# Four stages of a gated stack reordered: spline normalisation on VectorE, table rows by halves, and first similarities and one-hots taken earlier

## The chip, the cores and the metric

The kernel runs on one core of a Trainium2 chip. The metric is device time in microseconds (us), from the start of the launch to its end. Engines are named as the profile names them: PE (TensorE), PEld (its weight loads), DVE (VectorE), ACT (ScalarE), POOL (GpSimd) and SP (SyncE, which issues most transfers).

## What is computed

A stack of four layers, each with a mixer and a feed-forward block, on x of 8 x 256 x 512 floats. Every block adds tanh(gate) times its result of the layer-normalised x. The change touches the feed-forward of layer 1 (a spline layer), the mixer of layer 3 (a decaying state) and the feed-forward of layer 3 (retrieval by product keys):

```python
# _L1_ffn_ref, N = 2048 tokens, 64 tiles of 8 columns, 8 clusters
input_sigs = jnp.sign(xf)
cluster_scores = input_sigs @ cluster_sigs.T
tile_scores = input_sigs @ tile_sigs.T
tile_idx = jnp.argmax(jnp.where(in_cluster, tile_scores, -jnp.inf), axis=-1)
...
b = spline_bases[tile_idx[:, None], j, gi]
s = spline_slopes[tile_idx[:, None], j, gi]
delta = (b + s * x_local) * output_scale[tile_idx][:, None]
out = jnp.zeros_like(xf).at[jnp.arange(N)[:, None], tok_dims].set(delta)
...
# _L3_xattn_ref, after the scan
y = Z + summary
return (y - mu) / jnp.sqrt(var + LN_EPS) * gamma + beta
...
# _L3_ffn_ref
q = (x @ Wq).reshape(b, t, H, 2, DK)
sim1 = jnp.einsum('bthd,hkd->bthk', q1, keys[:, :, 0, :])
sim2 = jnp.einsum('bthd,hkd->bthk', q2, keys[:, :, 1, :])
s1, i1 = jax.lax.top_k(sim1, K)
...
w_down = e_down[final_indices]
w_up = e_up[final_indices]
hidden = jax.nn.silu(jnp.einsum('btd,bthkd->bthk', x, w_down)) * jax.nn.relu(final_scores)
out = jnp.einsum('bthk,bthkd->btd', hidden, w_up)
```

## The kernel before

The whole of x stays in SBUF as X, 16 tiles of 128 tokens by 512 columns. The kernel is a row of stages, each a function with its own buffers. At the end of a stage all engines meet, so that what is late on any of them delays all. `stats` carries the mean and the squared deviations of each row of X into the next stage. Stages, semaphores and the order on each engine are written out by hand; the order in the code is the order in the queue. `wait_ge(here(i, h))` in a loop means that turn i of buffer h has been filled, `before(i, h)` that its last use is over.

**Spline stage** (`spline_phase`, names with L1f, 596.8 to 718.2 us of the profile). DVE makes the row scale `r2` and shift `nm`. ACT normalises each tile into XN (L1583), four tiles ahead and then one between two sign operations (L1589). PE turns XN in chunks of four 128x128 transposes (L1514), ACT takes the sign of a turned chunk, and PE scores four tiles at a time against the tiles' signatures (L1522, 16 matmuls of 64 columns). DVE makes the one-hot OH of the chosen tile, eight tiles of X at a time (L1663 to L1671), and picks the eight chosen columns of each row, XS. PE turns the one-hots (L1540), ACT copies them to OHT (L1613), PE multiplies them with a table to fetch each token's row (L1546), and ACT copies the row to LUT (L1617); the two PSUM buffers of each are used in turn. PE does all 16 one-hots first, then all 16 rows. DVE's chain from L1683 on waits for the last row and has a long tail. At the end (the put loop) POOL spreads the result of a tile over 512 columns (L1502), DVE adds it to X (L1739) and makes the tile's statistics with bn_stats (L1743). ACT meanwhile is nearly idle.

**Decay stage** (`decay_phase`, L3x, 913 to 960 us). Each tile gets its layer norm, times gamma, plus beta. DVE makes z (L2051) and adds it to X with the row sum as a by-product; POOL has added beta to X before. ACT turns the row sum into the mean (L2004, a 128x2 copy) and then squares the deviations (L2010). PE is idle but for eight matmuls at the start.

**Route stage** (`route_phase`, L3r, 960 to 1098.8 us). DVE makes the row scale and shift of all 16 tiles with ACT's root between. Tiles go in eight pairs: ACT normalises two tiles (L2181), PE turns them, makes queries with Wq (L2155 and on) and similarities with the keys (L2167), ACT copies each result back, DVE takes the best eight of each of 8 rows of similarities (L2234) and goes on to the indices (`choose`). `mask` (L2219) and `keep_keys` (L2225), with POOL's `rank` and products between (L2135, L2139), belong to the pair before. At the end DVE makes the indices, weights `wts`, the statistics `stat`, and transposes FW, PH and PK.

**Retrieve stage** (`retrieve_phase`, L3f, 1099 to 1758 us). DVE splits the weights and x into high and low halves (`up_low` L2602, `down_low` L2598, `split_x` L2594), makes `xs` (L2659), and then one-hots of the chosen indices, 44 times (`one_hots`: one 128x512 compare, L2572, and four 128x128 ones, L2576). PE sums their products (L2419), and then come the hidden layer and the output in a long run of matmuls.

## Time and profile before

| | |
|---|---|
| median of 3 runs | 1764.09 us (1761.99 to 1770.47) |
| the profiled execution's own time | 1760.03 us |
| its span in the trace | 1758.3 us |
| mean granted TensorE clock, as a share of full speed | 0.892 |
| PE busy | 1363.1 us (78%) |
| DVE busy | 1424.3 us (81%) |
| ACT busy | 936.0 us (53%) |
| POOL busy | 545.6 us (31%) |

The busy times are averages over stages with different limits. The stages which the change touches take 121, 47, 139 and 659 us. The page's chain that ended last puts 24% of the span on PE and 6% on DVE, nearly all of it in the retrieve stage, and says nothing of the stages ahead; the rows of the timeline do. A row of the timeline joins instructions of one kind that follow each other on one engine: its duration runs from the first's start to the last's end.

### The profile page before, as it was taken

How to read it: one execution, taken by the hardware profiler on the slowest of the kernel's cores; microseconds unless marked ns; L12 is line 12 of the kernel's file. 1: busy time of each engine (PE TensorE's matmuls, PEld its weight loads, DVE VectorE, ACT ScalarE, POOL GpSimd, SP SyncE). 2: the span in 40 equal slices, each digit the busy share in tenths (PEclk: the TensorE clock that was granted, in tenths of full speed). 3: DMA queues.
4: the chain of work that ended last, by engine and by line, in shares of the span. 5: the costliest groups of instructions: out<-in, count | busy, mean ns of one | idle time of the engine just before them, and what ended most of it. 6: DMA issues, size and time to landing. Idle time of an engine off the chain costs nothing. (4 is left out here: it accounts for less than half of the span.)

```text
span 1758.3 us, 23962 instructions
## 1 busy us (share of the span) xinstructions
PE 1363.1 (78%) x6614; PEld 1011.7 (58%) x6614; DVE 1424.3 (81%) x3156; ACT 936.0 (53%) x1936; POOL 545.6 (31%) x569
## 2 busy tenths in 40 slices
PE   4889358886999667266771992489999899998888
PEld 2444224444788443254620882368888788876776
DVE  5999769985887468799488799888999889878785
ACT  3477646652333362466425441358888788733443
POOL 0000014442110022200013122214777577766541
PEclk8899779998999757688885996799999999999999
DMA  6230020000000210355200100416889799887974
GB/s 213 90 123 13 0 78 1 0 0 1 1 1 1 86 61 1 93 194 179 68 1 0 48 25 1 125 49 208 248 245 251 210 263 256 251 235 234 261 231 157
DMA packets 92286, 197.93 MB, mean 113 GB/s; under 512 B 16040, under 2 KB 25384, under 8 KB 91312
## 3 DMA queue, kind: packets, MB, share of 16 engines
q0 software_dynamic: 27120, 91.25, 18.9%
q1 hardware_dynamic: 65088, 105.82, 18.3%
q14 instruction: 51, 0.42, 0.1%
q8 instruction: 27, 0.44, 0.1%
HBM read 181.30 MB, written 15.73 MB: 112 GB/s over the span
## 5 line engine op out<-in xcount | busy, mean ns | idle before, releaser
L2379 POOL DMA_INDIRECT L3f_gd<-rows,idx x160 | 188.4, 1178 | 202.2 <-DVE L3f_gd L2608 177.0
L2379 POOL DMA_INDIRECT L3f_gu<-in_L_ffn_e_up,idx x160 | 168.4, 1052 | 71.2 <-issue 47.2
L2447 PE MATMUL L3f_o_ps<-L3f_euh,L3f_ath 128*128 128x512 f32 x352 | 146.4, 416 | 22.4 <-DVE L3f_atl L2589 19.5
L2435 PE MATMUL L3f_h_ps<-L3f_xh,L3f_edh 128*128 128x512 f32 (+1 forms) x384 | 144.0, 375 | 6.7 <-DVE L3f_xl L2594 6.7
L2419 PE MATMUL L3f_g_ps<-L3f_oh 128*128 128x128 f32 x704 | 97.0, 282 | 61.5 <-DVE L3f_oh L2576 61.5
L2435 PE MATMUL L3f_h_ps<-L3f_xh,L3f_edl 128*128 128x512 f32 (+1 forms) x384 | 144.0, 375 | 0.0
L2435 PE MATMUL L3f_h_ps<-L3f_xl,L3f_edh 128*128 128x512 f32 (+1 forms) x384 | 143.9, 375 | 0.0
L1030 POOL TENSOR_TENSOR wgu<-L0f_hid,magic 128x1408 bf16<-128x1408 f32 x16 | 45.2, 2825 | 315.2 <-DVE L0f_hid L1101 315.2
L2447 PE MATMUL L3f_o_ps<-L3f_eul,L3f_ath 128*128 128x512 f32 x352 | 138.9, 395 | 0.0
L2447 PE MATMUL L3f_o_ps<-L3f_euh,L3f_atl 128*128 128x512 f32 x352 | 138.9, 395 | 0.0
L2419 PEld LDWEIGHTS L3f_g_ps<-L3f_oh 128*128 128x128 f32 x704 | 90.9, 194 | 72.0 <-issue 67.4
L2622 DVE SCALAR_TENSOR_TENSOR X<-L3f_gu,L3f_coef,X 128x512 f32<-128x512 f32 x160 | 119.4, 747 | 0.7
L2491 ACT ACTIVATE L3f_at<-L3f_h_ps 128x512 f32<-128x512 f32 (+1 forms) x96 | 53.8, 560 | 116.3 <-PE L3f_h_ps L2435 77.7
L2585 DVE TENSOR_TENSOR L3f_at<-L3f_at,L3f_G 128x512 f32<-128x512 f32 (+1 forms) x96 | 62.1, 647 | 63.7 <-ACT L3f_at L2491 52.4
L2608 DVE SCALAR_TENSOR_TENSOR L3f_gd<-L3f_gd,L3f_xs 128x512 f32<-128x512 f32 x160 | 109.4, 685 | 0.0
L2447 PEld LDWEIGHTS L3f_o_ps<-L3f_euh,L3f_ath 128*128 128x128 f32 x352 | 66.8, 190 | 47.6 <-issue 36.8
L2512 ACT ACTIVATE L3f_oh<-L3f_oh,first,L3f_minus 128x128 f32<-128x128 f32 x216 | 89.2, 484 | 1.8
L2435 PEld LDWEIGHTS L3f_h_ps<-L3f_xh,L3f_edh 128*128 128x128 f32 x384 | 73.2, 191 | 18.4 <-DVE L3f_xl L2594 7.7
L2496 ACT ACTIVATE L3f_ath<-L3f_at 128x512 fp32r<-128x512 f32 (+1 forms) x96 | 57.3, 597 | 47.8 <-DVE L3f_at L2585 28.8
L2602 DVE TENSOR_TENSOR L3f_eul<-L3f_eu,L3f_euh 128x512 fp32r<-128x512 f32 x96 | 66.2, 690 | 18.5 <-ACT L3f_euh L2486 14.7
L2435 PEld LDWEIGHTS L3f_h_ps<-L3f_xl,L3f_edh 128*128 128x128 f32 x384 | 72.9, 190 | 10.8
L331 PE MATMUL L0x_vp_ps<-L0x_W,L0x_V 128*128 128x512 f32 x128 | 63.5, 643 | 20.0 <-ACT L0x_sv L491 20.0
(555 smaller groups left out, 3729.3 us busy)
## 6 DMA issues: line engine op xcount, KB each, us to landing
L3f_eu<-in_L_ffn_e_up SPq DMA_DIRECT2D x96, 256.0 KB
L3f_ed<-in_L_ffn_e_down SPq DMA_DIRECT2D x96, 256.0 KB
L2x_ed<-in_L_ffn_e_down SPq DMA_DIRECT2D x32, 256.0 KB, 3.3
rows<-L2x_eo SPq DMA_DIRECT2D x32, 256.0 KB, 2.4
wgu<-in_L_ffn_w_gate_upT SPq DMA_DIRECT2D x4, 1408.0 KB, 7.5
X<-in_x SPq DMA_DIRECT2D x4, 1024.0 KB, 10.2
L0x_V<-in_ctxT SPq DMA_DIRECT2D x8, 512.0 KB, 3.9
L1f_C<-in_ctx SPq DMA_DIRECT2D x2, 2048.0 KB, 12.9
```

Of the source, the lines that this page charges most:

```text
L331: last = pe.matmul(vp_ps[:, :], lhsT=V[b % 3][:, c, j * P:(j + 1) * P], rhs=W[:, c, D:2 * D], start=(c == 0), stop=(c == DC - 1))
L2379: pool.indirect_dma_start(buf[j % ND][:, :], None, table, bass.IndirectOffsetOnAxis(ap=idx[:, j:j + 1], axis=0)).then_inc(sem[j % ND], 16)
L2419: last = pe.matmul(g_ps[h][:, g, :], lhsT=oh2[h][:, g, :], rhs=oh1[h][:, g, :], start=True, stop=True)
L2435: last = pe.matmul(h_ps[h][:, 0:cols], lhsT=w[h][:, c, :], rhs=x[:, c, 0:cols], start=(c == 0 and m == 0), stop=(c == DC - 1 and m == 2))
L2447: last = pe.matmul(o_ps[a][:, :], lhsT=w[h][:, a * P:(a + 1) * P], rhs=x[h][:, :], start=False, stop=False)
L2491: act.activation(at[h][:, 0:cols], h_ps[h][:, 0:cols], ACT.Silu).then_inc(sl_ready, 1)
L2496: act.activation(ath[h][:, 0:cols], at[h][:, 0:cols], ACT.Copy).then_inc(ath_ready, 1)
L2512: last = act.activation(oh1[h][:, g, :], oh1[h][:, g, :], ACT.Relu, scale=minus[:, n * GR + g:n * GR + g + 1], bias=first[:, 1, n * GR + g ...
L2585: dve.tensor_tensor(ah, ah, Ge, ALU.mult).then_inc(at_ready, 1)
L2602: dve.tensor_tensor(eul[h][:, :], eu[h][:, :], euh[h][:, :].bitcast(F32), ALU.subtract).then_inc(eul_ready, 1)
L2608: dve.scalar_tensor_tensor(gd[j % ND][:, :], gd[j % ND][:, :], 1.0, xs[:, j // S, :], ALU.mult, ALU.mult, accum_out=hid[:, j:j + 1]).then_ ...
L2622: dve.scalar_tensor_tensor(X[:, TG + j // S, :], gu[j % ND][:, :], coef[:, j:j + 1], X[:, TG + j // S, :], ALU.mult, ALU.add).then_inc(add ...
```

## The change

Four stages are edited.

In the spline stage, normalising moves from ACT to DVE (a tensor_scalar), eight tiles straight after `nm` and eight after `sigs`. PE turns the first eight one-hots, fetches their rows, and then does the same with the second eight; the second row buffer is now `s_ps`, and ACT's copies follow the same order. In the put loop DVE's addition also gives the row sum; for 15 of the 16 tiles ACT makes the mean of it and squares the deviations, in place of bn_stats; the copy of `mean` stands at tile 8 of that loop.

```diff
-    l_ps = [t[:, :, :].rearrange("p t a -> p (t a)")[:, 0:TW] for t in ts_ps]
+    l_ps = [ts_ps[0][:, :, :].rearrange("p t a -> p (t a)")[:, 0:TW], s_ps[:, 0:TW]]
...
-            i, h = t // 2, t % 2
-            if t % 8 == 0:
-                pe.wait_ge(oh_made, 1 + t // 8)
-            pe.wait_ge(oht_ready, before(i, h))
-            pe.transpose(oh_ps[h], OH[:, t, :], ident[:, :]).then_inc(oh_turned, 1)
         pe.wait_ge(tab_in, 80)
-        for t in range(NT):
-            i, h = t // 2, t % 2
-            pe.wait_ge(oht_ready, here(i, h))
-            pe.wait_ge(lut_ready, before(i, h))
-            pe.matmul(l_ps[h], lhsT=OHT[:, t, :], rhs=TAB[:, :], start=True, stop=True).then_inc(l_ready, 1)
+        for k in range(2):
+            pe.wait_ge(oh_made, 1 + k)
+            for t in range(8 * k, 8 * k + 8):
+                i, h = t // 2, t % 2
+                pe.wait_ge(oht_ready, before(i, h))
+                pe.transpose(oh_ps[h], OH[:, t, :], ident[:, :]).then_inc(oh_turned, 1)
+            for t in range(8 * k, 8 * k + 8):
+                i, h = t // 2, t % 2
+                pe.wait_ge(oht_ready, here(i, h))
+                pe.wait_ge(lut_ready, before(i, h))
+                pe.matmul(l_ps[h], lhsT=OHT[:, t, :], rhs=TAB[:, :], start=True, stop=True).then_inc(l_ready, 1)
         pe.wait_ge(mm_made, 1)
         for k in range(2):
...
-        def normalise(t):
-            act.activation(XN[:, t, :], X[:, t, :], ACT.Identity, scale=r2[:, t:t + 1], bias=nm[:, t:t + 1]).then_inc(xn_ready, 1)
...
             for c in range(DC):
                 signs(g, c)
-                if g + 1 < NT // TG4:
-                    normalise(TG4 * (g + 1) + c)
...
+        for k in range(2):
+            with act.Fori(NP // 2 * k, NP // 2 * (k + 1)) as i:
+                for h in range(2):
+                    act.wait_ge(oh_turned, here(i, h))
+                    act.activation(OHT[:, 2 * i + h, :], oh_ps[h], ACT.Copy).then_inc(oht_ready, 1)
+            with act.Fori(NP // 2 * k, NP // 2 * (k + 1)) as i:
+                for h in range(2):
+                    act.wait_ge(l_ready, here(i, h))
+                    act.activation(LUT[:, 2 * i + h, :], l_ps[h], ACT.Copy).then_inc(lut_ready, 1)
...
+        for t in range(NT - 1):
+            act.wait_ge(x_ready, t + 3)
+            act.activation(stats[:, t, 1:5:3], rowsum[:, t:t + 1].to_broadcast([P, 2]), ACT.Copy, scale=1.0 / D).then_inc(mean_ready, 1)
+            act.wait_ge(mean_ready, t + 1)
+            if t >= 2:
+                act.wait_ge(dev_ready, t - 1)
+            act.activation(dev[t % 2][:, :], X[:, t, :], ACT.Square, scale=-1.0, bias=stats[:, t, 1:2],
+                           accum_out=stats[:, t, 2:3]).then_inc(dev_ready, 1)
+            if t == NT // 2:
+                act.wait_ge(proj, 1)
+                act.activation(mean[:, :], s_ps[0:B, :], ACT.Copy)
 
...
+        dve.wait_ge(nm_ready, 1)
...
+        def normalise(t):
+            dve.tensor_scalar(XN[:, t, :], X[:, t, :], r2[:, t:t + 1], nm[:, t:t + 1], ALU.mult, ALU.add).then_inc(xn_ready, 1)
...
+        for t in range(2 * TG4):
+            normalise(t)
...
+        for t in range(2 * TG4, NT):
+            normalise(t)
...
-        with dve.Fori(0, NP) as i:
-            for h in range(2):
-                t = 2 * i + h
-                dve.wait_ge(put_ready, here(i, h))
+        dve.memset(stats[:, 0:NT - 1, 5:6], 0.0)
+        for t in range(NT):
+            i, h = t // 2, t % 2
+            dve.wait_ge(put_ready, here(i, h))
+            if t < NT - 1:
+                dve.scalar_tensor_tensor(X[:, t, :], X[:, t, :], 1.0, sg[h][:, :], ALU.mult, ALU.add,
+                                         accum_out=rowsum[:, t:t + 1]).then_inc(x_ready, 1)
+            else:
                 dve.tensor_tensor(X[:, t, :], X[:, t, :], sg[h][:, :], ALU.add).then_inc(x_ready, 1)
-            for h in range(2):
-                t = 2 * i + h
-                dve.wait_ge(x_ready, here(i, h))
-                dve.bn_stats(stats[:, t, :], X[:, t, :]).then_inc(st_ready, 1)
+        dve.wait_ge(x_ready, NT + 2)
+        dve.bn_stats(stats[:, NT - 1, :], X[:, NT - 1, :]).then_inc(st_ready, 1)
```

In the decay stage POOL makes the means of 15 tiles (a 128x2 multiply by 1/512) behind its sixteen additions of beta. DVE makes the row statistics of the first four tiles ahead of the others. ACT and PE do the whole of the first pair's normalising, turning, queries and similarities in this stage; the PSUM banks of the spread summary are used again for it.

```diff
+    HT, EARLY, HD = NT // 2, 4, 4
...
+        pool.wait_ge(part_made, 1)
+        for t in range(NT - 1):
+            pool.wait_ge(x_ready, t + 1)
+            pool.tensor_tensor(stats[:, t, 1:5:3], rowsum[:, t:t + 1].to_broadcast([P, 2]), part[:, 0:1].to_broadcast([P, 2]),
+                               ALU.mult).then_inc(mean_ready, 1)
...
+        pe.wait_ge(y_ready, NT)
+        for h in range(2):
+            pe.wait_ge(xn_ready, h + 1)
+            for c in range(DC):
+                last = pe.transpose(t_ps[h][:, c, :], xn[h][:, c * P:(c + 1) * P], ident[:, :])
+            last.then_inc(turned, 1)
...
+            pe.wait_ge(xT_ready, h + 1)
+            for n in range(HD):
+                for c in range(DC):
+                    last = pe.matmul(q_ps[h][:, n, :], lhsT=Wq[:, c, n * P:(n + 1) * P],
+                                     rhs=queries[:, c, h * P:(h + 1) * P].rearrange("p (s a g) -> p a s g", s=8, a=4),
+                                     start=(c == 0), stop=(c == DC - 1))
+            last.then_inc(q_ready, 1)
...
+            pe.wait_ge(qT_ready, h + 1)
+            for n in range(HD):
+                last = pe.matmul(s_ps[h][:, 2 * n:2 * n + 2, :], lhsT=qT[h][:, n, :], rhs=Kd[:, n, :], start=True, stop=True)
+            last.then_inc(s_ready, 1)
...
-        for t in range(NT - 1):
-            act.wait_ge(x_ready, t + 1)
-            act.activation(stats[:, t, 1:5:3], rowsum[:, t:t + 1].to_broadcast([P, 2]), ACT.Copy, scale=1.0 / D).then_inc(mean_ready, 1)
+        def square_x(t):
...
+        for t in range(EARLY):
+            square_x(t)
+        act.wait_ge(st_ready, EARLY)
+        act.activation(hroot[:, :], stats[:, 0:EARLY, 2], ACT.Sqrt, scale=1.0 / D, bias=eps[:, 0:1]).then_inc(hroot_ready, 1)
+        for t in range(EARLY, NT - 1):
+            square_x(t)
+            if t == 6:
+                normalise(0)
+                normalise(1)
+            elif t == 7:
+                copy_turned(0)
+                copy_turned(1)
+            elif t == 10:
+                copy_query(0)
+            elif t == 12:
+                copy_query(1)
+            elif t == 13:
+                copy_sims(0)
+        copy_sims(1)
...
+        def begin_rows():
+            dve.wait_ge(st_ready, EARLY)
+            dve.tensor_scalar(hvar[:, :], stats[:, 0:EARLY, 2], 1.0 / D, LN_EPS, ALU.mult, ALU.add).then_inc(step, 1)
+            dve.tensor_copy(row[:, 0, 0:EARLY], stats[:, 0:EARLY, 1]).then_inc(step, 1)
...
+            dve.wait_ge(hroot_ready, 1)
+            dve.reciprocal(inv, hroot[:, :]).then_inc(step, 1)
...
+            dve.scalar_tensor_tensor(row[:, 2, 0:EARLY], row[:, 0, 0:EARLY], -1.0, inv, ALU.mult, ALU.mult).then_inc(row_ready, 1)
...
-        n = scale_y(0, n + 0)
-        for i in range(HT // 2):
+        n = scale_y(0, n)
+        for i in range(3):
             add_to_x(i)
+        begin_rows()
+        add_to_x(3)
+        n = end_rows(n)
         n = scale_y(1, n)
-        for i in range(HT // 2, HT):
+        for i in range(4, HT):
             add_to_x(i)
```

The route stage starts from the second pair; ACT normalises tiles 2 and 3 before the root of the other twelve, and DVE makes row statistics for those twelve alone. At its end, what doesn't depend on POOL's last products is put ahead of the waits for them. In the retrieve stage four `one_hots` stand ahead of or between the splits.

```diff
-        with pe.Fori(0, TG // 2) as i:
+        with pe.Fori(1, TG // 2) as i:
             pair(i, True, True)
...
+        for h in range(2):
+            normalise(2 + h, h)
+        act.wait_ge(asked, 1)
+        act.activation(root[:, EARLY:], var[:, EARLY:], ACT.Sqrt).then_inc(rooted, 1)
         act.wait_ge(nm_ready, 1)
-        for h in range(2):
-            normalise(h, h)
-        with act.Fori(0, NP - 1) as i:
+        with act.Fori(1, NP - 1) as i:
             pair(i, True)
         pair(NP - 1, False)
...
+        late = slice(EARLY, NT)
+        n = row_stats(dve, stats[:, late, :], m[:, late], var[:, late], w1[:, late], w2[:, late], step, 0)
...
+        link = linker(dve, chain)
+        link(dve.transpose(first[:, 1, :], FW[:, :, :].rearrange("p t s -> p (t s)")))
         dve.wait_ge(found, FS * (NP - 1) + 4)
         for j in range(2):
             mask(j)
+        link(dve.tensor_scalar(wts[:, :], FW[:, TG:NT, :].rearrange("p t s -> p (t s)"), tg[:, gate:gate + 1], None, ALU.mult))
+        for k, r in ((0, m), (1, rstd)):
+            link(dve.tensor_copy(stat[:, k, :], r[:, TG:NT]))
+        for a in range(4):
+            link(dve.memset(sec[a * 32:(a + 1) * 32, :], 32.0 * a))
         keep_keys(NP - 1)
         dve.wait_ge(keys_kept, 2 * NP)
-        link = linker(dve, chain)
-        for a in range(4):
-            link(dve.memset(sec[a * 32:(a + 1) * 32, :], 32.0 * a))
...
-        for r, dst in ((PH, first[:, 0, :]), (FW, first[:, 1, :]), (PK, M[:, :])):
+        for r, dst in ((PH, first[:, 0, :]), (PK, M[:, :])):
...
+        for h in range(2):
+            one_hots(h, h)
         up_low(0, 0)
+        down_low(0, 0)
         for h in range(2):
-            down_low(h, h)
+            one_hots(2 + h, h)
+        down_low(1, 1)
...
-        with dve.Fori(0, NP + 1) as i:
+        with dve.Fori(2, NP + 1) as i:
             for h in range(2):
                 one_hots(2 * i + h, h)
```

**DVE in the spline stage**, from the row shift `nm` to the first reduction of the scores (`CS`), in the kernel before and in the changed one:

```order
L1646 SCALAR_TENSOR_TENSOR L1f_nm<-L1f_m,L1f_r 128x16
L1647 TENSOR_SCALAR L1f_keep<-L1f_r,tg 128x16
L1648 TENSOR_TENSOR L1f_shift<-L1f_m,L1f_r 128x16
L1649 TENSOR_SCALAR L1f_shift<-L1f_shift,tg 128x16
L1652 TENSOR_REDUCE L1f_ss<-L1f_slopes 128x4
L1653 TENSOR_SCALAR L1f_ss<-L1f_ss 128x4
L1654 TENSOR_SCALAR L1f_ss<-L1f_ss 128x4
L1655 TENSOR_TENSOR L1f_ss<-L1f_ss 128x4
L1657 TENSOR_TENSOR L1f_sigs<-L1f_own,L1f_ss 128x256
L1663 TENSOR_REDUCE L1f_CS<-L1f_ts_ps 128x64
```

```order
L1650 SCALAR_TENSOR_TENSOR L1f_nm<-L1f_m,L1f_r 128x16
L1654 TENSOR_SCALAR L1f_XN<-X,L1f_r,L1f_nm 128x512 x8
L1658 TENSOR_SCALAR L1f_keep<-L1f_r,tg 128x16
L1659 TENSOR_TENSOR L1f_shift<-L1f_m,L1f_r 128x16
L1660 TENSOR_SCALAR L1f_shift<-L1f_shift,tg 128x16
L1663 TENSOR_REDUCE L1f_ss<-L1f_slopes 128x4
L1664 TENSOR_SCALAR L1f_ss<-L1f_ss 128x4
L1665 TENSOR_SCALAR L1f_ss<-L1f_ss 128x4
L1666 TENSOR_TENSOR L1f_ss<-L1f_ss 128x4
L1668 TENSOR_TENSOR L1f_sigs<-L1f_own,L1f_ss 128x256
L1654 TENSOR_SCALAR L1f_XN<-X,L1f_r,L1f_nm 128x512 x8
L1676 TENSOR_REDUCE L1f_CS<-L1f_ts_ps 128x64
```

The 16 normalisations stand ahead of the first reduction, eight of them ahead of the small operations that make `sigs`.

**ACT in the decay stage**, from the last root of the layer norm, in the kernel before, and from the first squares in the changed one:

```order
L2050 ACTIVATE L3x_root<-L3x_sq,L3x_eps 128x8
L2004 ACTIVATE stats<-L3x_rowsum 128x2
L2010 ACTIVATE L3x_dev,stats<-X,stats 128x512
L2004 ACTIVATE stats<-L3x_rowsum 128x2
L2010 ACTIVATE L3x_dev,stats<-X,stats 128x512
```

```order
L2057 ACTIVATE L3x_dev,stats<-X,stats 128x512 x4
L2079 ACTIVATE L3x_hroot<-stats,L3x_eps 128x4
L2057 ACTIVATE L3x_dev,stats<-X,stats 128x512 x3
L2062 ACTIVATE L3x_xn<-X,row 128x512 x2
L2057 ACTIVATE L3x_dev,stats<-X,stats 128x512
L2066 ACTIVATE queries<-L3x_bank 128x4x128 x2
L2057 ACTIVATE L3x_dev,stats<-X,stats 128x512 x3
L2070 ACTIVATE L3x_qT<-L3x_bank 128x512
L2057 ACTIVATE L3x_dev,stats<-X,stats 128x512 x2
L2070 ACTIVATE L3x_qT<-L3x_bank 128x512
L2057 ACTIVATE L3x_dev,stats<-X,stats 128x512
L2074 ACTIVATE sims<-L3x_bank 128x1024
```

The 128x2 copies have gone, and the first pair's normalising and its copies of turned tiles, queries and similarities stand between squares.

**DVE at the start of the retrieve stage**, from the negated weights `minus`, before and in the changed kernel:

```order
L2652 TENSOR_SCALAR L3f_minus<-first 128x352
L2602 TENSOR_TENSOR L3f_eul<-L3f_eu,L3f_euh 128x512
L2598 TENSOR_TENSOR L3f_edl<-L3f_ed,L3f_edh 128x512 x2
L2594 TENSOR_TENSOR L3f_xl<-L3f_xc,L3f_xh 128x512 x4
L2659 TENSOR_SCALAR L3f_xs<-X,stat 128x512 x5
```

```order
L2765 TENSOR_SCALAR L3f_minus<-first 128x352
L2685 TENSOR_TENSOR L3f_oh<-ident,second 128x512
L2689 TENSOR_SCALAR L3f_oh<-ident,first 128x128 x4
L2685 TENSOR_TENSOR L3f_oh<-ident,second 128x512
L2689 TENSOR_SCALAR L3f_oh<-ident,first 128x128 x4
L2715 TENSOR_TENSOR L3f_eul<-L3f_eu,L3f_euh 128x512
L2711 TENSOR_TENSOR L3f_edl<-L3f_ed,L3f_edh 128x512
L2685 TENSOR_TENSOR L3f_oh<-ident,second 128x512
L2689 TENSOR_SCALAR L3f_oh<-ident,first 128x128 x4
L2685 TENSOR_TENSOR L3f_oh<-ident,second 128x512
L2689 TENSOR_SCALAR L3f_oh<-ident,first 128x128 x4
L2711 TENSOR_TENSOR L3f_edl<-L3f_ed,L3f_edh 128x512
```

Two of the four early `one_hots` stand ahead of the first split, two ahead of the second `down_low`.

## Rows read from the trace of the kernel before

**Rows 1.** Timeline, spline stage's start: start us, us, engine, line, operation [idle before <-releaser]

```profile
602.27 2.93 ACT L1583 ACTIVATE L1f_XN<-X,L1f_nm,L1f_r 128x512 f32<-128x512 f32 x4 [1.57 <-DVE L1f_nm L1646]
...
605.25 3.16 PE L1514 MATMUL L1f_t_ps<-ident,L1f_XN 128*128 128x128 f32 x12 [10.31 <-ACT L1f_XN L1583]
...
619.85 0.63 PE L1522 MATMUL L1f_ts_ps<-L1f_sigs,L1f_sgT 128*128 128x64 bf16 x16
...
620.59 0.69 DVE L1663 TENSOR_REDUCE L1f_CS<-L1f_ts_ps 128x64 f32<-128x512 f32 x1 [16.54 <-PE L1f_ts_ps L1522]
```

**Rows 2.** Windows: us, busy us (count) of five engines, PE clock, DMA share, GB/s

```profile
612.00:617.00 5.00, 4.58 (x32) 4.10 (x32) 0.00 (x0) 3.79 (x7) 0.00 (x0) 0.50 1.05 387
617.00:624.00 7.00, 2.84 (x32) 2.27 (x32) 3.24 (x6) 6.25 (x10) 0.00 (x0) 0.99 0.79 293
```

**Rows 3.** Timeline, one-hots and table rows of the spline stage

```profile
629.02 1.63 ACT L1589 ACTIVATE L1f_sgT<-L1f_t_ps,L1f_bT,L1f_gT 128x512 bf16<-128x512 f32 x2 [0.98 <-PE L1f_t_ps L1514]
...
634.89 0.41 ACT L1613 ACTIVATE L1f_OHT<-L1f_t_ps 64x128 f32 x2
...
637.76 0.47 ACT L1613 ACTIVATE L1f_OHT<-L1f_t_ps 64x128 f32 x2 [0.49 <-PE L1f_t_ps L1540]
...
639.37 0.63 PE L1540 MATMUL L1f_t_ps<-ident,L1f_OH 128*64 128x128 f32 x2 [1.61 <-DVE L1f_OH L1671]
...
659.15 0.29 DVE L1683 TENSOR_TENSOR L1f_XS<-L1f_XS,L1f_LUT 128x128 f32<-128x128 f32 x1 [8.04 <-ACT L1f_LUT L1617]
```

**Rows 4.** Timeline, the put loop's first two pairs of tiles

```profile
692.92 2.04 DVE L1739 TENSOR_TENSOR X<-X,L1f_sg 128x512 f32 x2 [1.61 <-POOL L1f_sg L1502]
694.57 2.35 POOL L1502 TENSOR_TENSOR L1f_sg<-L1f_OH,L1f_DL 128x512 f32 x2 [0.76 <-DVE X L1739]
694.88 1.27 DVE L1743 BATCH_NORM_STATS2 stats<-X  x2
...
696.08 1.39 DVE L1739 TENSOR_TENSOR X<-X,L1f_sg 128x512 f32 x1
```

**Rows 5.** Decay stage: timeline; then the view of line L597

```profile
934.44 1.74 DVE L2051 SCALAR_TENSOR_TENSOR L3x_z<-L3x_Y,L3x_mid,gamma 128x512 f32<-128x512 f32 x1
...
946.47 0.17 DVE L2032 TENSOR_SCALAR L3x_var<-L3x_sq 128x8 f32<-128x8 f32 x1
...
L597 POOL TENSOR_TENSOR stats<-L2x_rowsum,L2x_part x7: 203/349/1198, 753.3 to 833.3; 128x4 f32<-128x4 f32 x7
```

**Rows 6.** Timeline, start of the route stage

```profile
960.02 0.19 DVE L100 TENSOR_TENSOR L3r_w<-stats 128x16 f32<-128x16 f32 x1 [0.94 <-PEq L88]
...
962.78 1.52 ACT L2181 ACTIVATE L3r_xn<-X,L3r_nm,L3r_rstd 128x512 f32<-128x512 f32 x2 [1.37 <-DVE L3r_nm L2215]
...
977.36 3.30 DVE L2234 MAX8 L3r_best<-L3r_sims 128x8 f32<-128x128 f32 x16 [14.61 <-ACT L3r_sims L2198]
...
977.95 1.03 ACT L2198 ACTIVATE L3r_sims<-L3r_s_ps 128x1024 f32<-128x1024 f32 x1 [0.70 <-PE L3r_s_ps L2167]
...
989.83 1.65 DVE L2234 MAX8 L3r_best<-L3r_sims 128x8 f32<-128x128 f32 x8 [1.04 <-ACT L3r_sims L2198]
```

**Rows 7.** Timeline, end of the route stage

```profile
1087.98 1.30 DVE L2219 TENSOR_TENSOR L3r_M<-L3r_rank,L3r_kio 128x512 f32<-128x512 f32 x2 [1.55 <-POOL L3r_rank L2135]
...
1090.43 0.69 DVE L2225 TENSOR_REDUCE L3r_PH<-L3r_M 128x64 f32<-128x512 f32 x1 [1.15 <-POOL L3r_M L2139]
...
1094.85 0.30 DVE L2287 TENSOR_SCALAR wts<-L3r_FW,tg 128x160 f32<-128x160 f32 x1
...
1096.34 0.71 DVE L2291 STREAM_TRANSPOSE first<-L3r_FW 128x512 f32<-128x512 f32 x1
```

**Rows 8.** Start of the retrieve stage: a window, then the timeline of DVE

```profile
1100.20:1107.80 7.60, 0.00 (x0) 0.00 (x0) 1.29 (x2) 2.87 (x6) 5.97 (x8) 0.50 0.95 340
...
1110.87 2.63 DVE L2659 TENSOR_SCALAR L3f_xs<-X,stat 128x512 f32<-128x512 f32 x5
1113.84 0.69 DVE L2572 TENSOR_TENSOR L3f_oh<-ident,second 128x512 f32<-128x512 f32 x1 [0.33 <-DVE L3f_xs L2659]
...
1165.12 0.68 DVE L2572 TENSOR_TENSOR L3f_oh<-ident,second 128x512 f32<-128x512 f32 x1
```

100 lines of the change are left out of this document (60 added, 40 removed).

## The prediction

> **What bounds the kernel now.** I read the page first: PE and DVE are each busy for some four fifths of the span, and the chain that ended last lies almost wholly in the retrieve stage. That says nothing of the earlier stages, since all engines meet at each stage's end. So I read the timeline of the four stages touched, looking at each place for the wait that ends last. In the spline stage's start it is DVE, idle 16.54 us until scores come [rows 1]: the loop of ACT's normalising and signs and PE's transposes. From there to the table's last row it is the ACT and PE exchange; DVE idles 8.04 us more [rows 3]. In the put loop it is POOL and DVE in turn [rows 4]. In the decay stage DVE sets the end, with ACT partly and PE wholly free. The route stage starts with DVE idle 14.61 us for similarities, and 1.04 us for the second pair's [rows 6]; its end has waits on POOL of 1.55 and 1.15 us [rows 7]. In the retrieve stage's first 7.6 us DVE is busy 1.29 [rows 8].
>
> **Terms against the profiled execution, 1760.03 us.**
>
> *A, spline front: −12.9.* ACT's four first normalises take 2.93 us and the first transposes start at 605.25 [rows 1]. DVE has made no such operation on these tiles; the nearest row is `xs`, the same shape with two scalars, 2.63 for 5 or 0.53 each [rows 8]. From 602.27 four of them end at 604.4, so transposes start at 604.45. The other twelve come every half microsecond, faster than a chunk of transposes, about 1.05 at the low clock (3.16 for three [rows 1]). `sigs` now comes behind eight normalises, at about 608.4, ahead of the first scores. Without normalises between them the signs are what ACT does: 0.71 apart once PE is fast, the pitch of ACT's 128x512 (2.93 / 4 is 0.73). The clock was .50 in 612 to 617 and .99 from 617 on, 4.9 us after the dense stretch of transposes and scores began at about 612.1 [rows 2]. The same density should now begin with the second chunk near 604.5, so I put the rise at about 609.4. Two groups' scores are then done at 604.45 + 5.0 + 5 × 0.71 + 2 × 0.63 = 614.3, and `CS` starts at 614.5 instead of 620.59 [rows 1]: 6.1 earlier for DVE. DVE's own chain to XS then ends at 651.1 (659.15 − 8.04 [rows 3]) − 6.1 = 645.0.
>
> On ACT and PE the last sign ends at about 619.0. Between the last sign and the first copy of a one-hot lie four moves of X and a table load, 4.24 us (630.65 to 634.89 [rows 3]), which stay: 623.2. Eight one-hot copies take 3.34 (634.89 to 638.23); from the second half's first transpose to the last row, eight transposes and sixteen table rows, it was 19.78 (639.37 to 659.15). The 1.61 us for which PE waited on DVE's second one-hots goes: by DVE's 6.1 they come at 633.3, and the first half's rows keep PE until 634.6. So 623.2 + 3.34 + 19.78 = 646.3, less 0.1 for transposes that slip in early, 646.2 against DVE's 645.0. XS starts 12.9 earlier. Splitting by halves is what lets the second one-hots be late by 10 us at no cost. What is late next is ACT and PE again. Bounds: −14 if DVE's end decides, −8 if the clock stays low (first rival).
>
> *B, put loop: −0.4.* A pair of tiles takes 3.16 us (692.92 to 696.08). After its second addition starts, POOL multiplies for 2.35 us for two tiles, and the next addition starts 0.2 after the first of them; the two bn_stats, 1.27, lie beside that multiply [rows 4]. DVE looks busy throughout, but in the first pair, ahead of which no bn_stats ran, the additions take the same 2.04 as later. So taking bn_stats out opens a gap on DVE and no more; only the last pair's statistics shorten, from 1.27 to one of 0.64, less what ACT's last square sticks out. An addition beside a multiply takes 1.39, the other 0.65 (2.04 − 1.39): they exclude each other. Bounds: −4.4 if bn_stats held the pair by half a microsecond each, +15.8 if without it every addition lands on a multiply (1.39 + 2.35 / 2 = 2.57 a tile, 41.1 for sixteen, against 8 × 3.16 = 25.3). I take the row of the first pair. The memset and the `mean` copy at tile 8 go beside it.
>
> *C, decay and route start: −8.4.* DVE's place for the row statistics is before the second `scale_y`, 946.47 [rows 5]. Two small operations (0.35) and six (0.21 apart, 1.25) follow, and the mean now comes by POOL. POOL's 128x2 multiply isn't in the trace; the nearest, 128x4 additions, take 0.203, 0.349 and 1.198 us at least, in the middle and at most [rows 5]; I take the middle, and 0.8 for one that meets a DVE instruction. The scale is ready at 946.47 + 0.35 + 1.25 + 0.8 = 948.9. The first pair's chain on ACT and PE took 16.2 us in the route stage (962.78 to 978.98 [rows 6]); with one square ahead of it, 0.8, it ends at 965.9. DVE's end was 959.08 (960.02 − 0.94), so the stage ends 6.8 later: PE has not been working before this chain, and neither had it there, so the same clock is assumed. Behind the meeting 0.94, then row statistics 2.75 (960.02 to 962.78), for twelve tiles as long as for sixteen, and 0.3 for the root behind two normalises: the best-eight search starts at 969.9 instead of 977.36, −7.5. ACT starts the second pair at 966.9; its first similarities are ready after 14.46 (962.78 to 977.25), at 981.3. DVE ends the first pair's choice at 969.9 + 11.43 (977.36 to 988.79) = 981.3. Both meet, against 989.83: −8.5, I take −8.4. The second scale_y and the later additions are pushed by 1.6 us; they end at 960.7, under cover of the chain to 965.9. Bounds: −5 if each of POOL's fifteen means stretches a square or a DVE instruction by 0.2, −11 if the chain runs at a faster clock.
>
> *D, route end: −1.9.* The 1.55 idle takes the transpose of FW, 0.71 and its link; the 1.15 takes `wts` 0.30, two copies of about 0.2 and the memsets [rows 7]: 0.75 + 0.33 + 0.41 + 0.44. If POOL is held up by them, nothing is gained on that part: −0.7.
>
> *E, retrieve start: −6.5.* One `one_hots` costs (1165.12 − 1113.84) / 31 = 1.65 with waits. Four of them, 6.5, go into 6.3 us of idle between 1100.2 and 1107.8 [rows 8]. The first split is pushed by about half a microsecond, what is behind it by up to 0.9, but the transfers it then waits for keep their times, so the later idle takes it up; and a wait of 0.7 for the first one-hots' matmuls goes too. The hidden layer's matmuls start behind the thirty-second one-hots and move by the same. Bounds: −4 if the splits' delay holds ACT and the transfers behind it, −7.3.
>
> Sum: −12.9 − 0.4 − 8.4 − 1.9 − 6.5 = −30.1, so 1729.9 for an execution like the profiled one. The median was 4.06 above it: **1734.0**.
>
> **Rivals.**
>
> *The clock stays low in the spline's start.* The stretch with .50 held transposes and one group of scores, and .99 came after [rows 2]; which of them raised it isn't told apart. If only the scores count, chunks of four go on at 1.05 and scores at about 1.06: the chain of signs ends 5.0 later, XS starts at 651.3, −7.9. That is 1739.0. Against it: the scores are few, and 4.9 us of mostly transposes sufficed. In a sentence apart: the Trainium skill ("TensorE: Matmul & The Clock Gate", section "Part 4: PE-mode transpose") says that transposes don't count as PE activity for the clock; the rise in rows 2 came after both kinds, so no row here contradicts it.
>
> *The put loop locks in step:* with nothing between, each addition meets a multiply, +15.8: 1749.8. For it: DVE would wait at the semaphore exactly when POOL starts. Against: the first pair. *Or it runs free:* −4.4, 1730.0; for it, DVE's row of busy time without a gap.
>
> *The chain in the decay stage is slower* (squares between, means late, a cold PE): −5 in place of −8.4, 1737.4.
>
> *Slower than before:* POOL's means lock DVE out. An operation there of 128x512 took 1.74 beside POOL's additions [rows 5], and 0.67 apart without. If each of the fifteen small means delays two such DVE instructions by that 1.07, it costs 32.1; with the locked put loop 47.9 is lost, and 1781.8 results. It decides from (30.1 − 15.8) / 15 = 0.95 us of delay per mean on. Against it: a mean lasts 0.35, and a lock can't outlast it by much.
>
> *It doesn't do what it says:* the instruction orders show every edit in place; what may be missing is that it is waited for elsewhere, which is the first rival.
>
> **How the numbers follow.** Forecast 0.45 (1731 to 1738); low clock 0.20; slower chain 0.15; free put loop 0.08; locked put loop 0.06; slower 0.03; other small misses of several terms together, ending between 1743 and 1762, 0.03. All cases except the last two lie 14 us or more below 1764.09. The range reaches down to 1725 (the bounds of A and C, −1.1 and −2.6, with the free put loop, −4.0) and up to 1748 (low clock, slower chain, D and E at their small ends: 5.0 + 3.4 + 1.2 + 2.5 = 12.1). Faster by over 0.5% (8.8 us, about what a measurement of this kernel can tell from no change) 0.93, within 0.04, slower 0.03.
>
> **What would show it.** A: `CS` near 614.5, XS near 646, no PE wait on the second one-hots, windows of clock .99 from 610. B: pairs still 3.1 apart and gaps on DVE where bn_stats was. C: the decay stage ends near 966 by page times shifted by A, ACT or PE last, and the first search starts about 4 us into the route stage. D: no idle of 1.55. E: `xs` ends where it did, and the next one-hots are the fifth. The forecast is wrong if XS moves by under 8, if additions in the put loop all take 1.39, or if DVE instructions in the decay stage's second half take over 0.75.

## The result, and the profile after

The changed kernel takes 1734.03 us (median of 4 runs, 1732.33 to 1735.17), the kernel before 1763.04 (4 runs, 1755.72 to 1770.47). The ratio is 0.9833, with a 95% interval of 0.980 to 0.9865. The two profiled executions are compared here: 1760.03 us before and 1732.33 after, with spans of 1758.3 and 1730.6, so 27.7 us less.

The stretches between fixed points on DVE's and PE's timelines, in us, before and after, with the change that was forecast:

| stretch | before | after | change | forecast |
|---|---|---|---|---|
| start to the spline stage | 597.12 | 598.87 | +1.75 | 0 |
| spline start to XS (term A) | 62.03 | 48.67 | −13.36 | −12.9 |
| XS to the put loop's first addition | 33.77 | 33.65 | −0.12 | 0 |
| put loop to the next stage (B) | 25.39 | 25.12 | −0.27 | −0.4 |
| two untouched stages | 194.71 | 194.68 | −0.03 | 0 |
| decay start to the second pair's first search (C) | 76.81 | 68.37 | −8.44 | −8.4 |
| from there to the last pair's ranks | 96.30 | 96.31 | +0.01 | 0 |
| ranks to the retrieve stage (D) | 13.72 | 13.11 | −0.61 | −1.9 |
| retrieve start to the first hidden-layer matmul (E) | 68.02 | 62.52 | −5.50 | −6.5 |
| from there to the span's end | 590.40 | 589.31 | −1.09 | 0 |

The spline stage's start in the timeline of the changed kernel, which answers to [rows 1] and [rows 3]; page times here are 1.75 later than before for the same point:

```profile
604.03 3.74 DVE L1654 TENSOR_SCALAR L1f_XN<-X,L1f_r,L1f_nm 128x512 f32<-128x512 f32 x8
...
606.00 5.91 PE L1516 MATMUL L1f_t_ps<-ident,L1f_XN 128*128 128x128 f32 x24 [9.32 <-DVE L1f_XN L1654]
...
611.74 0.63 PE L1524 MATMUL L1f_ts_ps<-L1f_sigs,L1f_sgT 128*128 128x64 bf16 x16
...
615.62 0.69 DVE L1676 TENSOR_REDUCE L1f_CS<-L1f_ts_ps 128x64 f32<-128x512 f32 x1 [2.38 <-PE L1f_ts_ps L1524]
...
624.84 0.41 ACT L1608 ACTIVATE L1f_OHT<-L1f_t_ps 64x128 f32 x2
...
647.54 0.29 DVE L1696 TENSOR_TENSOR L1f_XS<-L1f_XS,L1f_LUT 128x128 f32<-128x128 f32 x1 [1.43 <-ACT L1f_LUT L1612]
```

Eight normalises take 3.74 us on DVE, 0.47 each. DVE's wait ahead of `CS` has gone from 16.54 to 2.38 us and the one ahead of XS from 8.04 to 1.43. The windows around the first score (columns as in [rows 2]) show where the clock rises:

```profile
606.00:611.40 5.40, 5.21 (x22) 4.29 (x23) 5.19 (x17) 3.26 (x5) 0.00 (x0) 0.50 0.78 260
611.60:620.50 8.90, 7.48 (x91) 5.79 (x89) 6.31 (x11) 8.26 (x13) 0.94 (x1) 1.00 1.05 386
```

From 606.00 to 611.40 TensorE has run transposes and nothing else, at .50, its level of 1.2 GHz; from 611.60 on the window shows 1.00, full speed (2.4 GHz), and the first score comes only at 611.74.

The put loop, beside [rows 4]:

```profile
682.95 2.35 POOL L1504 TENSOR_TENSOR L1f_sg<-L1f_OH,L1f_DL 128x512 f32 x2 [0.77 <-DVE X L1753]
...
684.31 1.54 DVE L1753 SCALAR_TENSOR_TENSOR X<-X,L1f_sg 128x512 f32<-128x512 f32 x1 [0.95 <-POOL L1f_sg L1504]
...
687.42 1.54 DVE L1753 SCALAR_TENSOR_TENSOR X<-X,L1f_sg 128x512 f32<-128x512 f32 x1 [0.95 <-POOL L1f_sg L1504]
```

A pair takes 3.11 us, POOL's 2.35 is what it was, and where bn_stats stood DVE now waits 0.95 us for POOL. The addition beside a multiply lasts 1.54 us where it was 1.39, but it starts earlier beside it: in both kernels it ends 0.55 us after POOL's multiply (685.85 and 685.30 here; 697.47 and 696.92 in [rows 4]).

The decay stage's end and the route stage's start, beside [rows 5] and [rows 6]:

```profile
931.77 0.15 DVE L2147 TENSOR_SCALAR L3x_hvar<-stats 128x4 f32<-128x4 f32 x1
...
934.59 0.17 DVE L2153 RECIPROCAL row<-L3x_hroot 128x4 f32<-128x4 f32 x1
...
935.78 1.52 ACT L2062 ACTIVATE L3x_xn<-X,row 128x512 f32<-128x512 f32 x2 [0.22 <-DVE row L2163]
...
938.54 9.38 PE L2024 MATMUL L3x_bank<-queries,Wq 128*128 128x128 f32 x64
...
951.42 1.02 ACT L2074 ACTIVATE sims<-L3x_bank 128x1024 f32<-128x1024 f32 x1
...
953.05 1.52 ACT L2290 ACTIVATE L3r_xn<-X,row 128x512 f32<-128x512 f32 x2 [0.61 <-PEq L88]
...
953.38 0.18 DVE L100 TENSOR_TENSOR L3r_w<-stats 128x12 f32<-128x12 f32 x1 [5.11 <-PEq L88]
...
955.94 3.19 DVE L2346 MAX8 L3r_best<-sims 128x8 f32<-128x128 f32 x16
...
956.58 1.97 PE L2261 MATMUL L3r_t_ps<-ident,L3r_xn 128*128 128x128 f32 x8 [5.20 <-issue]
...
969.36 1.65 DVE L2346 MAX8 L3r_best<-sims 128x8 f32<-128x128 f32 x8 [2.10 <-ACT sims L2307]
```

DVE waits 5.11 us at the stage's end for the chain on ACT and PE, searches 2.56 us after the route stage's start, and then waits 2.10 for the second pair.

The route stage's end, beside [rows 7]:

```profile
1067.58 1.29 DVE L2331 TENSOR_TENSOR L3r_M<-L3r_rank,L3r_kio 128x512 f32<-128x512 f32 x2 [1.00 <-POOL L3r_rank L2244]
1068.36 2.86 POOL L2248 TENSOR_TENSOR L3r_M<-L3r_M,L3r_I 128x512 f32<-128x512 f32 x2 [0.88 <-DVE L3r_M L2331]
1068.80 1.30 DVE L2390 TENSOR_SCALAR wts<-L3r_FW,tg 128x160 f32<-128x160 f32 x1
1070.13 1.32 DVE L2392 COPY stat<-row 128x5 f32<-128x5 f32 x2
```

`wts` took 0.30 before and takes 1.30 here; two copies of five columns take 1.32. Both run beside a product of POOL.

### The profile page after: what moved, and what is told of

Same layout as the page of the kernel before. It is cut to its first block and busy times, and to the rows that moved or that the text cites. A ratio compares the mean times of both kernels' runs of the same rounds, so it can differ in the third digit from the quotient of the medians.

```text
span 1730.6 us, 23911 instructions
## 1 busy us (share of the span) xinstructions
PE 1359.7 (79%) x6594; PEld 1010.3 (58%) x6614; DVE 1427.6 (82%) x3181; ACT 936.4 (54%) x1951; POOL 559.0 (32%) x585
```

## The experiments

All kernels are edits of the changed one. They were measured in four groups, each beside its own runs of the kernel before. The medians of that kernel differ by up to 8 us between the groups (1763.97, 1755.75, 1756.80, 1761.93), so times are compared as ratios to it, whose intervals are about ±0.002 to ±0.003, or 3 to 6 us. What is smaller is read from the stretches of the trace, in us. The first two and the one from the ranks on repeat within 0.2 us over the kernels that leave them as they are; the other two repeat less well, since the clock and the landing of a transfer move them: the changed kernel itself gave 68.37 and 69.21 for the one, 62.52 and 63.00 for the other.

| kernel | ratio | spline to XS | put loop | decay to 2nd search | ranks to retrieve | retrieve to matmul |
|---|---|---|---|---|---|---|
| changed | 0.9833 | 48.67 | 25.12 | 68.37 | 13.11 | 62.52 |
| changed again | 0.9837 | 48.64 | 25.12 | 69.21 | 13.13 | 63.00 |
| put loop back | 0.9841 | 48.66 | 25.39 | 68.36 | 13.12 | 62.23 |
| 16 and 16 back | 0.9886 | 54.85 | 25.10 | 68.38 | 13.12 | 63.72 |
| normalise on ACT | 0.9907 | 60.35 | 25.11 | 68.35 | 13.12 | 62.59 |
| means on ACT | 0.9850 | 48.74 | 25.12 | 69.34 | 13.12 | 62.50 |
| no early pair | 0.9886 | 48.60 | 25.10 | 79.21 | 13.11 | 62.47 |
| wts, stat back | 0.9855 | 48.70 | 25.11 | 68.44 | 12.59 | 62.44 |
| one-hots back | 0.9876 | 48.60 | 25.09 | 68.48 | 13.12 | 69.16 |
| warm spline | 0.9842 | 47.80 | 25.10 | 68.46 | 13.13 | 62.50 |
| rows sooner | 0.9833 | 48.60 | 25.12 | 67.33 | 13.11 | 62.42 |
| warm decay | 0.9855 | 48.60 | 25.10 | 67.61 | 13.11 | 63.99 |
| joined | 0.9810 | 47.82 | 25.12 | 67.23 | 12.58 | 61.74 |

**The put loop back**, to an addition and bn_stats for each tile:

```diff
-                dve.scalar_tensor_tensor(X[:, t, :], X[:, t, :], 1.0, sg[h][:, :], ALU.mult, ALU.add,
-                                         accum_out=rowsum[:, t:t + 1]).then_inc(x_ready, 1)
+                dve.tensor_tensor(X[:, t, :], X[:, t, :], sg[h][:, :], ALU.add).then_inc(x_ready, 1)
...
+                dve.bn_stats(stats[:, t, :], X[:, t, :]).then_inc(st_ready, 1)
```

> The changed kernel with the put loop as it was: bn_stats on DVE for all tiles, ACT idle. Theory (POOL's multiply and DVE's addition in turn are the cycle, bn_stats lay in DVE's gap): pairs of tiles stay 3.1 us apart, DVE's idle of 0.95 a pair becomes bn_stats, the loop to the next stage's start is 25.4 us instead of 25.1, and the time is 0.3 us above the changed kernel's 1734.0. Rival (bn_stats was the bound, since DVE looked busy throughout): pairs 3.65 apart with it or the changed loop would have been shorter by as much, 4.4 us above.

The loop takes 25.39 us, to a hundredth what it was before the change, and pairs are 3.11 apart. The ratio is above by more than that (0.9841 for 0.9833), within the interval. bn_stats lay in a gap. POOL's two multiplies take 2.35 us with it and 2.35 without: it never held POOL up. By the rule of the Trainium skill on the shared ports, quoted in the prediction ("SBUF — State Buffer", section "SBUF: two separate sides"), an operation with one input wouldn't, and the trace agrees.

**All sixteen one-hots first** (with ACT's copies in the same order):

```diff
+        for k in range(2):
             for t in range(8 * k, 8 * k + 8):
                 i, h = t // 2, t % 2
                 pe.wait_ge(oht_ready, here(i, h))
```

> The changed kernel with all sixteen one-hots turned ahead of the sixteen table rows again; normalising stays on DVE. Theory (with ACT and PE early, DVE's second one-hots are late, and the halves hide that): DVE's second one-hots are ready at 634.3 in the changed kernel's trace, PE waits there some 6 us with eight one-hots turned, and the last row comes 19.8 us later, XS at 655.0 instead of 647.5: 7.5 us more, 1741.5. Rival (the exchange of ACT and PE is the chain in either order): XS within 0.6 us of 647.5, time within 1 us.

XS comes 6.2 us later, for 7.5 expected. PE's timeline has the wait, and XS follows 19.6 us after its end:

```profile
633.18 0.64 PE L1543 MATMUL L1f_t_ps<-ident,L1f_OH 128*64 128x128 f32 x2 [6.81 <-DVE L1f_OH L1685]
```

**Normalising back on ACT:**

```diff
+                if g + 1 < NT // TG4:
+                    normalise(TG4 * (g + 1) + c)
...
-        for t in range(2 * TG4):
-            normalise(t)
```

> The changed kernel with the normalising back on ACT between its signs; the halves stay. Theory (normalising is what kept ACT from the signs and with them the transposes at the low clock): the first copy of a one-hot goes from 624.8 back to 636.6, and as the rows follow it without a wait on DVE, XS comes 11.8 us later, at about 659.3; 1745.8. Rival (the halves carry most of the gain): XS 2 to 4 us later, 1738.

XS comes 11.68 us later, as the theory had it. The two edits together: from the stretch of before, 62.03, the halves alone take 1.68 (to 60.35), DVE's normalising alone 7.18 (to 54.85), both 13.36. A third of the gain, 4.5 us, belongs to neither alone: with ACT and PE early, DVE's second one-hots become the late part, and the halves hide just that.

**One-hots back behind the splits:**

```diff
-        for h in range(2):
-            one_hots(h, h)
         up_low(0, 0)
...
-        with dve.Fori(2, NP + 1) as i:
+        with dve.Fori(0, NP + 1) as i:
```

> The changed kernel with the retrieve stage's DVE order as it was: splits and xs first, then all 44 one-hots. Theory (four one-hots went into idle time of DVE): from the negated weights to the first hidden-layer matmul 68.0 us again instead of 62.5, time 5.5 above, 1739.5. Rival (that stretch moved for another reason, the transfers' times say): within 1 us of 1734.

The stretch is 69.16, for 68.0 expected: 6.6 more than in the changed kernel and 1.1 more than in the kernel before, whose DVE order this is. The second `down_low` tells why:

```profile
1087.65 0.69 DVE L2711 TENSOR_TENSOR L3f_edl<-L3f_ed,L3f_edh 128x512 fp32r<-128x512 f32 x1 [4.52 <-ACT L3f_edh L2594]
```

It starts 9.03 us behind the negated weights (1078.62); in the kernel before it was 7.96 (1107.81 − 1099.85). It waits for ACT's high half of the same weights, and that one for their transfer, which lands later by that much. With four one-hots in front DVE reaches this operation 8.8 us behind the negated weights, so a wait up to then costs nothing. In two other kernels it could start only at 10.5 us (warm decay) and 10.15 (16 and 16 back), and their stretch is 63.99 and 63.72.

**Means on ACT, POOL idle:**

```diff
-        for t in range(NT - 1):
-            pool.wait_ge(x_ready, t + 1)
-            pool.tensor_tensor(stats[:, t, 1:5:3], rowsum[:, t:t + 1].to_broadcast([P, 2]), part[:, 0:1].to_broadcast([P, 2]),
-                               ALU.mult).then_inc(mean_ready, 1)
...
+            act.activation(stats[:, t, 1:5:3], rowsum[:, t:t + 1].to_broadcast([P, 2]), ACT.Copy, scale=1.0 / D).then_inc(mean_ready, 1)
```

> The changed kernel with the decay stage's means made by ACT again (128x2 copies with a scale ahead of each square), POOL idle behind its additions. Theory (POOL's means are beside the chain and slow DVE's small operations only): the copies add 15 times 0.2 us to ACT, which has idle time until the last three of its steps; the scale of the first rows is ready up to 0.5 us earlier, and the first search of the route stage starts within 0.6 us of where it did; time within 1 us of 1734. Rival (each of POOL's means holds DVE up): stage shorter by 15 times 0.2 to 0.7, so 3 to 10 us faster.

The first search comes 0.2 us sooner, 54.76 for 54.95: POOL's means, 1.31 us for two, hold nobody up. The second pair's comes 0.97 later, 14.6 us behind the first for 13.4, and that goes with the clock: it rose 8.8 us into the route stage here and 6.4 in the changed kernel. The changed kernel's own second profile shows the same without any edit. First the profile shown above, then the second one, with a window on each side of the rise and TensorE's query matmuls:

```profile
956.50:959.70 3.20, 3.10 (x13) 2.71 (x14) 3.20 (x18) 1.60 (x3) 0.00 (x0) 0.50 0.00 0
959.90:968.00 8.10, 8.10 (x68) 7.92 (x67) 7.36 (x62) 1.99 (x4) 0.57 (x2) 1.00 0.35 130
...
958.56 7.97 PE L2269 MATMUL L3r_q_ps<-queries,Wq 128*128 x64
```

```profile
956.40:963.00 6.60, 5.79 (x26) 5.40 (x27) 6.57 (x42) 2.60 (x4) 0.00 (x0) 0.50 0.29 108
963.20:968.00 4.80, 4.80 (x45) 4.80 (x45) 4.67 (x43) 0.60 (x1) 0.04 (x1) 1.00 0.16 59
...
959.18 9.25 PE L2269 MATMUL L3r_q_ps<-queries,Wq 128*128 x64
```

The 1.28 us more for the queries are the whole difference between 13.42 and 14.70. Over the kernels whose first pair is early (but for joined, where TensorE's order differs), the second search comes 13.4 us behind the first where the rise is 6.4 to 6.5 us into the stage, 14.07 at 7.8, and 14.6 to 14.7 at 8.8 to 9.1. Since the same kernel shows both ends, a difference of that kind can't be put down to an edit.

**No early pair**, with the decay stage and the route stage's start of before (`decay_phase` and `route_phase` up to the last `choose` as they were):

```diff
-        with pe.Fori(1, TG // 2) as i:
+        with pe.Fori(0, TG // 2) as i:
             pair(i, True, True)
```

> The changed kernel with the decay stage and the route stage's start as they were (first pair in the route stage, means on ACT); the route stage's end, spline and retrieve parts stay. Theory: from the decay stage's first instruction on DVE to the second pair's first search 76.8 us again instead of 68.4; 8.4 us above, 1742.4. Rival (the gain is given back within the route stage, whose later pairs are bound by DVE anyway): 1 us or less above, 1735.

The stretch is 79.21, for 76.8 expected: 10.8 more than in the changed kernel and 2.4 more than the same code took in the kernel before. Of these, 1.65 us are in the decay stage itself (48.64 us long for 46.99), and their reason stands on DVE beside POOL's additions of beta:

```profile
905.76 19.66 POOL L1992 TENSOR_TENSOR X<-X,beta 128x512 f32<-128x512 f32 x16 [3.70 <-DVE L3x_Y L2042]
...
916.61 8.84 DVE L2047 TENSOR_SCALAR L3x_var<-L3x_sq 128x8 f32<-128x8 f32 x1
```

An operation on eight columns took 8.84 us: it ended when the last of POOL's sixteen additions did. In the two profiles of before and after it got between two additions (0.44 and 0.29). The other 0.76 fall between the route stage's start and the first search, where the clock rose 10.1 us into the stage for 8.5 in the kernel before. So the part is worth 8.4 or 10.8 by what the old code happened to meet.

**wts and stat behind the products:**

```diff
-        link(dve.tensor_scalar(wts[:, :], FW[:, TG:NT, :].rearrange("p t s -> p (t s)"), tg[:, gate:gate + 1], None, ALU.mult))
-        for k, r in ((0, m), (1, rstd)):
-            link(dve.tensor_copy(stat[:, k, :], r[:, TG:NT]))
         for a in range(4):
```

> The changed kernel with wts and the two copies of stat behind POOL's products again, where they stood; the transpose of FW and the memsets stay early. In the changed kernel's trace wts takes 1.30 and the two copies 1.32 us beside POOL's products, against 0.30 and 0.38 before. Theory (each waits for a product of POOL to end, since both read SBUF): the reduction of M starts 1.7 us sooner, at the end of POOL's product, the three cost 0.75 behind it, and the time is about 0.6 us less than 1734.0. Rival (the trace stretches them because the wait for POOL is put inside them, and nothing is lost): 0.7 us more, 1734.7.

```profile
1069.35 0.69 DVE L2337 TENSOR_REDUCE L3r_PH<-L3r_M 128x64 f32<-128x512 f32 x1 [0.85 <-POOL L3r_M L2248]
...
1073.24 0.30 DVE L2400 TENSOR_SCALAR wts<-L3r_FW,tg 128x160 f32<-128x160 f32 x1
1073.57 0.38 DVE L2402 COPY stat<-row 128x5 f32<-128x5 f32 x2
```

The stretch is 0.52 us shorter, and `wts` is at 0.30 again; the ratio, 0.9855, is too coarse for it. That piece of the change lost time. In the changed kernel `wts` ended 0.1 us after POOL's first product and the first copy with its second (1070.10 for 1070.00, 1071.24 for 1071.22), so DVE waited inside them; here the reduction of PH runs beside POOL's second product and keeps its 0.69. The Trainium skill ("SBUF — State Buffer", section "SBUF: two separate sides") names fast modes of VectorE as taking the ports shared with GpSimd for the whole instruction. These rows agree with a lock of that kind; whether `wts` and the copies run in such a mode, no row shows.

**Transposes ahead in the spline stage:**

```diff
+        for j in range(16):
+            pe.transpose(s_ps[:, 0:P], ident[:, :], ident[:, :])
         for g in range(NT // TG4):
```

> The changed kernel with sixteen transposes of the identity in TensorE's idle time ahead of the spline stage's first transposes; they write a PSUM bank that is used later and change no result. In the changed kernel's trace the granted clock is .50 from 601.2 on and rises at 611.5, 5.5 us after transposes began at 606.0, with no other matmul before it. Theory (transposes raise the clock, and what matters is when they start): the clock is at full level soon after 606, chunks of four go at ACT's pace of 0.77 instead of 1.02, the first six chunks save about 1.5 us, and XS comes 1.5 us sooner; 1732.5. Rival (transposes by themselves don't raise the clock, and the rise had another cause): it rises at 611.5 as before, XS unmoved, 1734.

```profile
600.40:606.10 5.70, 5.44 (x24) 4.85 (x24) 5.09 (x17) 0.77 (x2) 0.00 (x0) 0.50 0.33 13
606.30:612.00 5.70, 4.89 (x46) 3.62 (x47) 5.09 (x15) 5.35 (x9) 0.00 (x0) 0.99 0.91 325
```

The clock is at .50 to 606.1 and full from about 606.4, with transposes and nothing else from 600.44 on, and XS comes 0.87 us sooner, not 1.5. The 1.5 counted all six chunks ahead of the first score at the fast pace, but the first two, from 604.33 on, still ran at the low clock.

**The first rows' scale sooner:**

```diff
         begin_rows()
+        n = end_rows(n)
         add_to_x(3)
-        n = end_rows(n)
```

> The changed kernel with the six operations of the first rows' scale straight behind the two that begin it, one pair of additions sooner, and the first pair's normalising and copies two squares sooner in ACT's order. In the changed kernel's trace the root is ready at 931.1, the two operations start at 931.77, and the six wait behind a pair of additions until 934.59. Theory (this chain alone sets the stage's end, since DVE idles 5.1 us there): normalising starts at 933.1 instead of 935.78, the chain and with it both first searches of the route stage come 2.7 us sooner: 52.3 us instead of 54.95 from the decay stage's start to the first search; 2.7 us less in all. Rival (ACT's squares, which follow DVE's additions, hold the copies back): 1 us or less.

The chain starts 2.7 us sooner, as expected, but two of ACT's squares now stand between its last two copies, and the first search comes at 52.75 us for 54.95, 2.2 sooner. The second comes 1.0 sooner: the clock rose 8.8 us into the route stage.

**Matmuls of constants ahead of the first pair's chain:**

```diff
+        pe.wait_ge(x_ready, 4)
+        for j in range(8):
+            pe.matmul(bank[:, B - 1, :], lhsT=ident[:, :], rhs=Wq[:, 0, 0:D], start=True, stop=True)
```

> The changed kernel with eight 128x512 matmuls of constants on TensorE ahead of the first pair's transposes in the decay stage, released by the fourth tile's addition; they write a PSUM bank that is free there and change no result. In the changed kernel's trace the granted clock rises at 942.58, 5.8 us after the chain began at 936.7; the 64 query matmuls take 9.38 us there and 7.41 in the route stage at the full clock. Theory (the chain pays for TensorE's low clock): the clock is up near 936, queries take 7.4, transposes 1.1 instead of 1.9; both first searches come 2 to 2.8 us sooner. Rival (the rise doesn't come sooner, or ACT's squares hold the copies anyway): within 0.5 us.

```profile
926.51 8.66 PE L2017 MATMUL L3x_bank<-Wq,ident 128*128 128x512 f32 x16 [15.11 <-DVE X L2143]
...
935.00 1.04 PE L2021 MATMUL L3x_bank<-ident,L3x_xn 128*128 128x128 f32 x8
...
936.29 7.41 PE L2027 MATMUL L3x_bank<-queries,Wq 128*128 128x128 f32 x64 [0.25 <-ACT queries L2069]
```

Transposes 1.04 for 1.94, queries 7.41 for 9.38, as expected; but the constants hold the transposes to 935.00, 1.2 us after the first tile is normalised (933.8), and the first search is 1.4 us sooner, for 2 to 2.8 expected. The second is 0.8 sooner, with the clock's rise 7.8 us into the route stage.

**Joined**: `wts` and `stat` behind the products, the transposes in the spline stage, the first rows' scale sooner, the constants in the decay stage, and in the route stage TensorE's clearing of semaphores last:

```diff
-        ph.tidy(pe)
+        for j in range(4):
+            pe.transpose(t_ps[0][:, 0, :], ident[:, :], ident[:, :])
```

> The changed kernel with five things together: wts and stat behind POOL's products, matmuls of constants ahead of the chains in the spline and decay stages, the first rows' scale and copies sooner, and in the route stage TensorE's clearing of semaphores (which held its first transposes back to 956.58, 2.7 us after their tiles were normalised) at the end of its work instead of the start, with four transposes of the identity ahead. Theory (each stretch pays for itself, and the later rise of the clock in the route stage ate 1.16 and 0.65 us of the two single edits in the decay stage): spline to XS 47.8 us instead of 48.7, from the decay stage's start to the second pair's first search 63 to 64 us instead of 68.4, route's end 12.6 instead of 13.1; 6 to 7 us less than the changed kernel run beside it. Rival (the clock's rises come late again in the route stage and the search is bound by it): second search at 66 us or later, 3 to 4 us less.

> The changed kernel itself, on the same chip as the one before. Its stage lengths should repeat within 0.2 us where no transfer is waited for (spline to XS 48.7, put loop 25.1, decay to second search 68.4, route's end 13.1), and only the stretches ahead of the spline stage and behind the first hidden-layer matmul should differ by microseconds; 1.5 to 1.9% less than the kernel before.

The changed kernel's second profile kept that to 0.1 us in three stretches, but for the second search it has 69.21 and not 68.4, as read above.

```profile
930.35 8.67 PE L2019 MATMUL L3x_bank<-Wq,ident 128*128 128x512 f32 x16 [15.10 <-DVE X L2145]
938.85 1.04 PE L2023 MATMUL L3x_bank<-ident,L3x_xn 128*128 128x128 f32 x8
...
954.37 1.97 PE L2267 MATMUL L3r_t_ps<-ident,L3r_xn 128*128 128x128 f32 x8
```

The rows are the joined kernel's. It takes 1729.61 us against 1734.51 for the changed kernel beside it, with ratios of 0.9810 (0.9786 to 0.9834) and 0.9837 (0.9814 to 0.9860): less by 4.9 us in the medians, where 6 to 7 were expected, and with intervals that overlap. The stretches that the edits touch carry 3.3 us of it: spline 0.8, route's end 0.5, decay to second search 2.0, the last with the rise of the clock in it. The theory wanted 4.4 to 5.4 in that last one; 67.23 is the rival's case (66 or later). The rows show what went wrong: the tiles were ready from 934.9 on and PE was still at the constants until 938.85. Two edits that each paid for themselves got in each other's way: the first search comes 54.3 us into the decay stage, where it came at 52.75 and 53.54 with one of them. The clearing of semaphores is confirmed as a cost: with it moved, the tiles' transposes start 0.1 us after their tile (954.37 for 953.42 + 0.81), where they were 2.7 late.

## Why the prediction was right, point by point

**A.** Each step held, once 1.75 is taken from the page times: transposes from 604.25 (said 604.45), the rise of the clock at 609.9 (609.4), `CS` at 613.87 (614.5), the first copy at 623.1 (623.2), XS at 645.8 (646.2). What the prediction left unsaid was how the gain splits; the two undone kernels show it.

**The low clock** was the strongest rival and is refuted: it rose with transposes alone, twice. The Trainium skill's rule ("TensorE: Matmul & The Clock Gate", section "Part 4: PE-mode transpose") says they don't count; the trace doesn't agree, and the measurement decides.

**B.** −0.27 for −0.4, by the reason given: POOL's multiplies and DVE's addition in turn set the pair. Neither put-loop rival came: additions beside a multiply take 1.54, the others 0.68, in turn as before.

**C.** The sum was right to 0.04 us and several of its steps were not. The chain started 34.8 us into the decay stage (935.78 − 900.99), where 35.9 was said: the two small operations (931.77) and POOL's mean stood ahead of the fourth pair of additions, and only the six that follow (934.59) were waited for. It took 16.7 us for 17.0 and so ended 51.45 us into the stage (951.42 + 1.02 − 900.99), where 52.9 was said. Behind the meeting the row statistics of twelve tiles took 2.56 us for 3.05. So the first search gained 9.4 us and not 7.5. The second pair then took 16.3 us from its normalising (953.05 to 969.36), where 14.46 was said. Its transposes started 3.5 us behind ACT's first normalise, where they started 0.9 behind it in the kernel before:

```profile
963.72 1.97 PE L2151 MATMUL L3r_t_ps<-ident,L3r_xn 128*128 128x128 f32 x8 [37.63 <-ACT L3r_xn L2181]
```

TensorE was still clearing semaphores when its tiles were ready, which the prediction put at nothing; in the kernel before that work was over by the time the tiles came. From the transposes on, the pair took 12.8 us for 13.6, so the clock wasn't to blame in this profile: it rose 3.2 us behind their start, for 4.8 before. The errors cancel, which is luck.

**D.** Wrong in size: −0.6 for −1.9. The step that failed is "the 1.15 takes `wts` 0.30, two copies of about 0.2 and the memsets": `wts` and the copies take 1.30 and 1.32 beside POOL's products. The low bound, −0.7, came near, but for the other side of the lock: it had POOL held up by them, and POOL's products take 2.86 us for 2.87 before, while DVE was held up. With `wts` and the copies put back the gain is 1.1.

**E.** −5.5 for −6.5. Against its own undoing it is worth 6.6. The comparison with before is smaller since the second e_down transfer landed earlier there by 1.1 us (7.96 for 9.03).

**The slower rival** needed a delay of 0.95 us for each of POOL's means. DVE's additions beside them take 0.74 to 0.75, as before. DVE can be held for longer than one of POOL's instructions, though (8.84 us in no early pair), which the prediction's argument against this rival didn't allow for.

**The sum.** The touched stretches give −28.2, for −30.1 forecast; the spans −27.7, with +1.75 ahead of the change and −1.09 behind it. That the median came out at 1734.03 for 1734.0 is luck to that extent: the last stretch alone, which no kernel here edits, is between 584.7 and 595.4 us long from one profile to the next, the two untouched stages between 193.5 and 196.1, and the spline stage starts between 596.2 and 600.2.

## What to carry to other kernels

Look for the wait that ends last in each stage, and ask of two edits in one stage what each is worth without the other: here a third of the spline gain exists only with both. Idle time spent waiting for a GpSimd product isn't free for every operation: here a scaling and a copy lasted until the product ended (1.30 us for 0.30, 1.11 for 0.17), while bn_stats and a reduction beside one kept their 0.7. A term that comes out to the hundredth may be two errors, so compare its steps and not only its sum.

## What the runs showed of the hardware that was not expected

- TensorE's clock rose to full speed (2.4 GHz) during transposes alone: by 611.6 where they began at 606.00, and by 606.4 where they began at 600.44.
- In the route stage the rise came between 6.4 and 9.1 us behind the stage's start for the same instructions, and moved the second pair by up to 1.3 us.
- A DVE addition that meets a multiply of POOL ended 0.55 us after it in all eight pairs, whether it started 0.07 us into it (changed kernel) or 0.24 (before): its length (1.54 or 1.39) tells when it started and not what it costs.
- A DVE operation on 128x8 was held for 8.84 us, over several of POOL's additions, and not for one.
- TensorE's clearing of semaphores at a stage's start held its first transposes back 2.7 us.
